# Transformer block on one core: the issue order of weight reads, unit maxima and last stores around the change from projections to attention

## The reference

```python
x = x + _layernorm(attn(_layernorm(x), Wq, bq, Wk, bk, Wv, bv, Wo, bo, gq, gk))
x = x + _layernorm(ffn(_layernorm(x), W_base, b_base, W_gate, W_thr, b_thr, A, B))

# attn
q = rms_norm(hidden @ Wq + bq, gq); k = rms_norm(hidden @ Wk + bk, gk); v = hidden @ Wv + bv
attn = softmax(einsum('bhqd,bhkd->bhqk', q, k) / sqrt(128))
out = einsum('bhqk,bhkd->bhqd', attn, v) @ Wo + bo
```

## Time and profile before

| | us |
|---|---|
| median of 3 runs | 1089.0 (1088.1 to 1089.79) |
| the profiled execution's own time | 1089.79 |
| its span | 1088.0 |
| TensorE busy | 1064.9 (98%) |
| DVE busy | 796.6 (73%) |
| ACT busy | 722.6 (66%) |
| POOL busy | 677.7 (62%) |

### The profile page before, as it was taken

The page is one execution under the profiler, slowest core; times in us unless marked ns, Lnnn a source line. Parts: engine busy times, 40 slices in busy tenths (PEclk is TensorE's granted clock), DMA queues, the critical chain, the costliest instruction groups (busy, mean ns, idle before and its releaser), DMA issues.

```text
span 1088.0 us, 19818 instructions
## 1 busy us (share of the span) xinstructions
PE 1064.9 (98%) x5781; PEld 580.3 (53%) x5781; DVE 796.6 (73%) x1802; ACT 722.6 (66%) x1427; POOL 677.7 (62%) x592
## 2 busy tenths in 40 slices
PE   7999999999999999999999999999999999999896
PEld 4444444444444655555555555555555555555385
DVE  8866666666655887777777777777777777777886
ACT  4775665656656787767677677676776777766432
POOL 2776766667667476667667666676676666764413
PEclk9999999999999999999999999999999999999999
DMA  6799999898984588866767667667666676765502
GB/s 240 190 216 272 224 208 226 187 231 200 221 178 155 149 216 223 202 174 175 186 164 189 174 161 191 182 160 179 186 175 174 175 190 162 186 155 151 152 1 78
DMA packets 311639, 197.43 MB, mean 181 GB/s; under 512 B 275248, under 2 KB 279216, under 8 KB 311472
## 3 DMA queue, kind: packets, MB, share of 16 engines
q1 hardware_dynamic: 311600, 196.97, 70.3%
HBM read 94.14 MB, written 35.68 MB: 119 GB/s over the span
## 4 chain that ended last, share of the span: by engine, by line
PE 61%; issue 15%; POOL 14%; DVE 5%; ACT 1%; DMA 1%; SPq 1%; POOLq 1%; DVEq 0%
PE ps L1120 20%; PE ps L1122 20%; PE ps L1121 20%; POOL acc L605 11%; POOL qk_out L596 3%; DVE stats L1471 1%; DMA qk_in<-x 1%; DVE y L1960 1%; ACT pair_q L947 1%; ACT ps L938 0%; DVE ps L1863 0%; POOL acc L651 0%; DMA pair_k<-pair_q 0%; DMA y<-x 0%; DVE y L1846 0%
## 5 line engine op out<-in xcount | busy, mean ns | idle before, releaser
L1863 DVE TENSOR_SCALAR_CACHE_REDUCE ps<-ps,score_down 128x512 f32<-128x512 f32 x256 | 177.5, 756 | 94.7 <-PE ps L1122 94.1
L1877 DVE SCALAR_TENSOR_TENSOR pair_q<-ps,row_inv,pair_q 128x512 f16<-128x512 f32 x256 | 174.5, 745 | 55.3 <-ACT pair_q L947 55.3
L938 ACT ACTIVATE ps<-ps,neg_max 128x512 f32<-128x512 f32 x256 | 168.3, 657 | 45.5 <-DVE ps L1863 45.4
L1120 PE MATMUL ps<-xh,wa_hi 128*128 128x512 f16 x512 | 194.5, 380 | 1.8 <-DVE wa_lo L1576 1.8
L1122 PE MATMUL ps<-xh,wa_lo 128*128 128x512 f16 x512 | 194.6, 380 | 0.0
L1121 PE MATMUL ps<-xl,wa_hi 128*128 128x512 f16 x512 | 194.5, 380 | 0.0
L699 POOL CAST oth<-o_t 128x512 f16<-128x512 f32 x62 | 37.8, 610 | 211.0 <-ACT o_t L923 211.0
L947 ACT ACTIVATE pair_q<-ps,row_inv 128x512 f16<-128x512 f32 x256 | 154.9, 688 | 20.8 <-DVE row_inv L1870 20.8
L605 POOL TENSOR_TENSOR acc<-acc,squares 128x512 f32<-128x512 f32 x120 | 150.6, 1276 | 0.0
L1122 PE MATMUL ps<-wv_hi,xl 128*128 128x256 f16 x512 | 139.6, 273 | 0.0
L1121 PE MATMUL ps<-wv_lo,xh 128*128 128x256 f16 x512 | 139.6, 273 | 0.0
(11 more groups left out here) (189 smaller groups left out, 2242.4 us busy)
## 6 DMA issues: line engine op xcount, KB each, us to landing
q_k_scratch<-qk_out SPq DMA_DIRECT2D x64, 512.0 KB, 8.1
qk_in<-q_k_scratch SPq DMA_DIRECT2D x64, 512.0 KB, 3.3
wa_stage<-w_qk SPq DMA_DIRECT2D x32, 512.0 KB, 5.8
u_stage<-w_vo SPq DMA_DIRECT2D x32, 512.0 KB, 6.9
wv_stage<-w_vo SPq DMA_DIRECT2D x16, 512.0 KB, 4.5
wo_stage<-w_vo SPq DMA_DIRECT2D x16, 512.0 KB, 4.5
qk_tops<-qk_top_scratch SPq DMA_DIRECT2D x28, 128.0 KB, 5.2
y<-x SPq DMA_DIRECT2D x8, 256.0 KB, 5.1
```

The source lines that it names most:

```text
L938: act.activation(ps[:, SCORE + i, :], ps[:, SCORE + i, :], ACT.Exp, bias=neg_max[:, sl, i:i + 1], scale=-1.0, accum_out=row_sum[:, sl, i:i ...
L1120: pe.matmul(outp, lhs[0], rhs[0], start=first, stop=False)
L1863: dve.tensor_scalar(ps[:, SCORE + i, :], ps[:, SCORE + i, :], score_down[:, sl, i:i + 1], None, ALU.mult, ALU.min, accum_out=neg_max[:, sl ...
L1877: dve.scalar_tensor_tensor(out=pair_q[:, 1, i, :], in0=ps[:, SCORE + i, :], scalar=row_inv[:, sl, i:i + 1], in1=pair_q[:, 0, i, :], op0=AL ...
```

## The change

Three things change, all of them in the order of work on SP and DVE. No arithmetic is changed, and no tensor; ACT, POOL and TensorE keep their programs.

1. Units. Before, SP reads a second unit in heads 4, 5 and 6 (`more=2`, `more=3`), and runs three units ahead of the head from then on, DVE two ahead (`unit=3` on SP, `unit=2` on DVE). Now the loops over heads 2 to 25 read unit h+1 and reduce unit h, and the two missing units are made up at the end: SP reads a second unit in heads 27 and 28, DVE reduces a second one in heads 27 and 28, right behind the second `store_k`.
2. The first loads of `wv_stage` and `wo_stage` move from heads 6 and 8 to before and behind head 26, and the store of `top_v` (with its wait) from before head 26 to behind head 27; the load of `tops_v` from behind head 27 to behind head 28.
3. In phase B `load_wv(0)` moves from behind step 3 of pair 0 into that step, and the last three stores of q and k from pair 1 into steps 2 and 3 of pair 0, the wait for all stores from before pair 2 to before pair 1.

```diff
-            def phase_a(i, o, weights=True, tops=True, top=True, unit=3, more=None):
+            def phase_a(i, o, weights=True, tops=True, top=True, unit=1, more=None):
...
-            phase_a(1, 0, unit=1, more=2)
-            phase_a(1, 1, unit=0, more=2)
-            phase_a(2, -2, unit=2, more=3)
-            sp.dma_start(wv_stage[:, :, :].rearrange("p c n -> p (c n)"), w_vo[0]).then_inc(wv_loaded, 16)
...
-            with sp.Fori(3, PAIRS // 2 - 1) as i:
+            with sp.Fori(1, PAIRS // 2 - 1) as i:
                 for o in range(-2, 2):
                     phase_a(i, o)
+            sp.dma_start(wv_stage[:, :, :].rearrange("p c n -> p (c n)"), w_vo[0]).then_inc(wv_loaded, 16)
+            phase_a(PAIRS // 2 - 1, -2)
+            sp.dma_start(wo_stage[:, :, :].rearrange("p h n -> p (h n)"), w_vo[PAIRS]).then_inc(wo_loaded, 16)
+
+            phase_a(PAIRS // 2 - 1, -1, weights=False, more=2)
             sp.wait_ge(v_top_ready, 1)
             sp.dma_start(vo_top_scratch[0], top_v[:, :]).then_inc(v_top_stored, 16)
-            phase_a(PAIRS // 2 - 1, -2)
-            phase_a(PAIRS // 2 - 1, -1, weights=False)
+            phase_a(PAIRS // 2 - 1, 0, weights=False, top=False, unit=2, more=3)
             sp.wait_ge(v_top_stored, 16)
             sp.dma_start(tops_v[:, :], vo_top_scratch[0:1].broadcast_to([P, P])).then_inc(v_tops_loaded, 16)
-            phase_a(PAIRS // 2 - 1, 0, weights=False, top=False)
             phase_a(PAIRS // 2 - 1, 1, weights=False, top=False, tops=False, unit=0)
...
@@ DVE
-            def phase_a(i, o, top=True, unit=2, more=None):
+            def phase_a(i, o, top=True, unit=0, more=None):
...
             largest_value()
             phase_a(PAIRS // 2 - 1, -2)
-            phase_a(PAIRS // 2 - 1, -1)
-            phase_a(PAIRS // 2 - 1, 0, top=False)
+
+            phase_a(PAIRS // 2 - 1, -1, more=1)
+            phase_a(PAIRS // 2 - 1, 0, top=False, unit=1, more=2)
             value_factors()
             value_biases()
-            phase_a(PAIRS // 2 - 1, 1, top=False)
+            phase_a(PAIRS // 2 - 1, 1, top=False, unit=2)
...
@@ SP, phase B
-                if s == 0:
-                    store_last(0)
-            load_wv(0)
-            for s in range(4):
-                step(1, s)
-                if s > 0:
-                    store_last(s)
+
+                for k in ((0,), (), (1, 2), (3,))[s]:
+                    store_qk(HEADS - 2 + k % 2, k % 2, k // 2, 2 * HEADS - 3 + k)
```

More of the change, by code:

```diff
@@ L440, in _ @@
             store_qk(1, 1, 1, 4)
-            phase_a(1, -2, unit=1)
-            phase_a(1, -1, unit=1)
-            phase_a(1, 0, unit=1, more=2)
-            phase_a(1, 1, unit=0, more=2)
-            phase_a(2, -2, unit=2, more=3)
-            sp.dma_start(wv_stage[:, :, :].rearrange("p c n -> p (c n)"), w_vo[0]).then_inc(wv_loaded, 16)
[L448 to L451, removed]
-            with sp.Fori(3, PAIRS // 2 - 1) as i:
+            with sp.Fori(1, PAIRS // 2 - 1) as i:
                 for o in range(-2, 2):
                     phase_a(i, o)
+            sp.dma_start(wv_stage[:, :, :].rearrange("p c n -> p (c n)"), w_vo[0]).then_inc(wv_loaded, 16)
+            phase_a(PAIRS // 2 - 1, -2)
+            sp.dma_start(wo_stage[:, :, :].rearrange("p h n -> p (h n)"), w_vo[PAIRS]).then_inc(wo_loaded, 16)
+            phase_a(PAIRS // 2 - 1, -1, weights=False, more=2)
             sp.wait_ge(v_top_ready, 1)
             sp.dma_start(vo_top_scratch[0], top_v[:, :]).then_inc(v_top_stored, 16)
-            phase_a(PAIRS // 2 - 1, -2)
-            phase_a(PAIRS // 2 - 1, -1, weights=False)
+            phase_a(PAIRS // 2 - 1, 0, weights=False, top=False, unit=2, more=3)
             sp.wait_ge(v_top_stored, 16)
             sp.dma_start(tops_v[:, :], vo_top_scratch[0:1].broadcast_to([P, P])).then_inc(v_tops_loaded, 16)
-            phase_a(PAIRS // 2 - 1, 0, weights=False, top=False)
             phase_a(PAIRS // 2 - 1, 1, weights=False, top=False, tops=False, unit=0)
@@ L482, in _ @@
                 load_qk(0, s)
[L484 to L491, removed]
             def load_wo(p):
@@ L506, in step @@
                         load_wo(p)
-                    if s == 3 and weights and not first:
-                        load_wv(p)
+                    if s == 3 and weights:
+                        sp.wait_ge(wv_lo_ready, 2 * p + 4)
+                        sp.dma_start(wv_stage[:, :, :], w_vo[bass.ds(p + 2, 1)].rearrange(
+                            "a p (c n) -> p (a c) n", c=C)).then_inc(wv_loaded, 16)
                 sp.wait_ge(high_ready, 4 * n + 4)
@@ L535, in _ @@
                     sp.wait_ge(stored[par][b], 16 * PAIRS)
-            with sp.Fori(2, PAIRS - 2) as p:
+            with sp.Fori(1, PAIRS - 2) as p:
                 for s in range(4):
@@ L1759, in phase_a @@
                         largest_of_unit(h + more, (par + more) % 2, 16 * (2 * i + (o + more) // 2 + 1))
-            phase_a(1, -2, unit=0)
-            phase_a(1, -1, unit=0)
-            phase_a(1, 0, unit=0)
-            phase_a(1, 1, unit=0, more=1)
-            phase_a(2, -2, unit=1, more=2)
-            for o in range(-1, 2):
-                phase_a(2, o)
-            with dve.Fori(3, PAIRS // 2 - 1) as i:
+            with dve.Fori(1, PAIRS // 2 - 1) as i:
                 for o in range(-2, 2):
```

## The result

| us | before | after |
|---|---|---|
| median of 4 runs each, same chip | 1088.55 (1087.78 to 1089.79) | 1098.82 (1096.85 to 1100.51) |
| the profiled execution's own time | 1089.79 | 1100.07 |
| its span | 1088.0 | 1098.2 |

The ratio is 1.0093 (95% interval 1.0073 to 1.0112): slower by 10.3 us, 2.0 us above the forecast and inside the range.

The account below looks back on a forecast made before the run. TensorE, busy 98% of the span, was taken as the bound, waiting at phase A's end on a DVE-ACT-POOL chain without slack. 1089.8 + 7.8 = 1097.6, with the median 0.8 lower at 1096.8; range 1090.6 to 1101.5 us.

Parts of the forecast that it names:

- The mechanism: End of phase A: DVE's factors of head 31 start 7.8 us late, delaying ACT, POOL and TensorE: +7.8 us.
- The load of `tops_v`: Behind head 28: issued at 326.0, landing 7.6 us later at 333.6, making DVE's factors of head 31 7.8 us late.
- both waits end together: SP before the `tops_v` load: landing of `top_v`'s store (325.6) and wait for POOL's low half (326.0) end together.
- The second unit of head 28: DVE in head 28: its 1.21 us reduction lies within the wait for `tops_v`, so it is free.
- Unit 28: Head 27: issued at 308.3, lands 6.9 us later, reduced at 316.4, DVE's factors of head 30 0.65 us early.
- rival 2: Unit 28 lands after 12.9 us, DVE's head 28 is 5.3 us late, TensorE stops in head 29: 1102.8; chance 0.12.
- The low clock: End of phase A: a lower-clock stretch between head 31 and the column sums takes 1.7 us, hidden by 2.4 us.
- Kept as before: Behind the column sums: the 1.7 us cost of the lower clock stays, since TensorE still idles ahead of them.
- the second stop of TensorE at the column sums: Sign: after idling 5 to 7 us ahead of head 31, TensorE is idle again at the column sums.
- the 2.4 us in which TensorE was to wait for POOL: Column sums: TensorE would be there at 348.5, POOL releases them at 350.9.
- Phase B: Pair 0: stores and loads ahead of the transposes leave TensorE 2.6 us of room: 0 us, at most 1.
- The early heads: Heads 4 to 8: fewer units and loads bring 0, as TensorE waits for nothing there.

Follow-up runs that it names:

- the chain alone: Only the store of `top_v` moved behind head 27 and load of `tops_v` behind head 28: ratio 1.0052 to the kernel before; with maxima stored first, 1089.45 us.
- second chip: Series running the kernel after again (1122.41 us), variants with DVE's waits moved, and the kernel before with the maxima stored first (1087.59 us); kernel before 1111.17 us.
- third chip: Series of parts of the change, each added to the kernel before with the maxima stored ahead of weights and unit; the kernel before takes 1092.2 us.
- all parts: The kernel after with the store of the maxima ahead of the loads of weights and unit: 1094.15 us, ratio 1.0026 to the kernel before.
- first chip: Series of single parts of the change, each made alone in the kernel before, which takes 1111.9 us there.
- the stand-in above: Kernel before with maxima stored first and units late, used in place of the unrun kernel with maxima stored first alone: 1087.34 us, ratio 0.9964.

## Why the prediction was right, and where a term was off

**The mechanism, right.** DVE's factors of head 31 set ACT, POOL and the end of phase A, and they were to start 7.8 us late: measured 8.92. Head 31 was to start 6.8 us later than in the earlier trace rows, and starts 8.04 us later, for the same reason. Taking DVE's waits out of the way takes the stop from 8.60 us to 1.03 and gives back 6.0 of 11.2 us, and the chain alone makes a wait for `tops_v` on each of two chips: that these waits make the stop is shown. For the rest of the 10.3 us see below.

**The load of `tops_v`, right in sum only.** Its issue was put at 326.0 and was 330.03: the store was issued at 314.68, not 313.0, and landed after 15.3 us, not the 12.6 of the earlier trace rows. The landing of the load took 4.6 us, not the 7.6 of the earlier trace rows. The end was forecast for 333.6 and came at 334.66. The sentence that "both waits end together" was wrong: the landing of the store ended last. That 333.6 came so near is luck: 4.0 us too early against 3.0 us too long. The Trainium skill's rule ("DMA: Bandwidth & Descriptors", section "Anatomy of one DMA — SWDGE (gpsimd) path"), by which the load would take 2.15 us (an estimate by that page), does not fit the 4.6 either. The page states it for a DMA that GpSimd issues; this one is SP's.

**The second unit of head 28, free as forecast, but not its traffic.** DVE waited 4.48 us for it, a wait the prediction did not have, and was done with it at 332.08, 2.6 us before `tops_v`. Moved out of the way (second chip) it gave 1.0 us, within the intervals. What was left out is that both late units stand in the queues beside the store of `top_v`: on the third chip, with all parts in place of the chain alone, the same store took 2.4 us more and the load 0.9. That may be the source of the 15.3 us here in place of 12.6, but isn't shown: on the first chip the same store took 13.8 us with the chain alone and 16.1 and 16.3 in two kernels whose units are as before.

**Unit 28, right in the first comparison.** Its maximum was to be done at 316.4, and began at 316.43: SP issued the unit at 310.87, not 308.3, and it landed in 5.4 us, not 6.9. So the factors behind it are 0.5 us late in place of 0.65 early. TensorE in head 29 doesn't stop for it. On the first chip DVE waited 8 us for it and rival 2's stop was there: its mechanism holds where phase A is already behind, and is no part of the result predicted.

**The low clock, off by its place.** "Kept as before" failed, and so did the second stop of TensorE at the column sums that the prediction named as a sign. The low stretch moved up, into the three products ahead of the column sums, which took 10.6 us for the 7.8 forecast, and none was left behind them. That used up the 2.4 us in which TensorE was to wait for POOL. Head 31 starts 8.04 us late, the column sums 9.48, and the next product but one behind them 7.7 (357.80 against 350.10). The errors cancel: 1.7 us more than forecast at the column sums, against 1.8 us of low clock behind them that went. At the end of phase A the kernel was 7.7 us late for the forecast's 7.8, and that it fits so well is luck.

**Phase B, mis-sized.** Put at 0, at most 1. The part costs 1.3 us where it can be read (third chip), by the stand-in above. The transposes of step 3 stood behind four transfers: the first took 7.1 us to land there and 7.6 on the first chip, for the 3.9 of the earlier trace rows. What the prediction left out is SP's own time. The issue of the first took 4.9 and 5.3 us, not 1.62, and the second was issued 3.3 and 3.7 us later for it. The room was 2.6 us, and on the third chip TensorE waited 0.78 us. In the profiled execution of the kernel after this is mostly hidden, because TensorE is already late by the 1.89 us of step 2. That wait comes and goes: a kernel with phase B as before has it in its profile, and one with the changed phase B hasn't, so it isn't shown to be the change's.

**What is left.** 7.7 us at the end of phase A and 1.5 in step 2 (1.89 in place of 0.38) make 9.2. The last 1.0 is the low clock behind the stop at 1043.39 shown above. The kernel before had the same stop and kept its clock, so this too isn't shown to be the change's. The prediction had neither. How much of these 2.5 us the median of the four runs holds isn't known: the runs of the kernel after spread over 3.7 us.

**The early heads** cost 0, as forecast: the first loads of `wv_stage` and `wo_stage` alone have the ratio 0.9986 (0.9967 to 1.0004), and in the first comparison TensorE has no stop in heads 2 to 26 of the kernel after.

## What to carry to other kernels

A small result that goes through DRAM and back should be stored as early as it exists and read behind work that others wait for; moving its store by two heads and its load by one turned a round trip that was done 2.8 us ahead of its reader into 7.1 us of waiting on DVE and 7.5 on TensorE. Put the small transfer whose landing is awaited ahead of the bulk loads in the same queue: one such swap was worth 23.6 us (2.1%) where the loop was behind, more than all that the change did. Where two waits stand in a row on one engine, removing the first shows the second at full length, so price them together.

## What the runs showed of the hardware

- The store of 128 x 4 bytes (`top_v`) took 8.5 to 17.5 us to land in the traces of these kernels. It was not measured by itself: in the kernel after, the 512 KB store issued just ahead of it took 14.2 us too, and the one before that 8.2. In the kernel before the DMA engines moved 110 GB/s at a share of 0.99 from 302 to 307 us, while it was on its way, but they also moved only 114 GB/s at 0.85 from 287 to 292, ahead of its issue. What makes it slow stays open.
- The kernel before takes 1088.55, 1092.2, 1111.17 and 1111.9 us in four series, while the one with the store of the maxima first takes 1087.59 in one of the slow ones. What differs between the series is not in the traces, and chip and time aren't separated. What the traces show is that DVE waits 55.0 us for the maxima in the kernel after there, and 6.0 with the edit.
- The same stop of TensorE was followed by the lower clock in one trace and not in another: 3.09 us, then 0.53 and 0.61; 3.00 us, then 1.00.
- The first DMA transpose of a step (`pair_k<-pair_q`) took SP 1.6 us to issue and landed 3.9 us after that began (medians of the kernel before). Behind two stores and two loads of 512 KB it took 4.9 to 5.6 us to issue and 7.1 to 7.7 to land.
- With the granted clock at 1.2 GHz, a 128x512 matmul behind a long stop took 0.59 to 0.63 us in place of 0.38.
